# A graph-attention layer and a routed expert layer in one kernel: first loads reordered, the router folded into the projections, the routing steps moved apart

## What is computed

```python
h = (xn @ W).reshape(N, 8, 256)                       # xn = layernorm(x), W 256 x 2048
e = leaky_relu(a_src[src] + a_dst[dst], 0.2)          # a_src, a_dst = h . att, one number per head
alpha = exp(e - max over dst) / sum over dst
x1 = x + segment_sum(h[src] * alpha, dst).mean(heads) + bias
t = layernorm(x1)
probs = softmax(t @ router_w.T)                       # 8 experts, the best two with weights rw
out = x1 + t + sum over the two of rw * (gelu(t @ w1[e] + b1[e]) @ w2[e] + b2[e])
```

## Time and profile before

| What | Value |
|---|---|
| median of 3 runs | 999.45 us |
| lowest and highest | 999.15 and 1000.62 us |
| the profiled execution, its time | 1001.77 us |
| the profiled execution, its span | 1000.0 us |
| busy PE, DVE, POOL, ACT | 680.0, 680.9, 638.1, 355.0 us |
| mean granted clock of PE | 0.806 of full speed |
| bytes moved | 189.66 MB, 190 GB/s |

### The profile page before, as it was taken

How to read it: one execution, slowest core, us unless ns; L and a number is a source line. 1 busy time by engine, 2 the same in 40 slices (tenths; PEclk the granted TensorE clock), 3 DMA queues, 4 the chain that set the end, 5 groups by cost and what they waited for, 6 DMA issues and landing times.

```text
span 1000.0 us, 16168 instructions
## 1 busy us (share of the span) xinstructions
PE 680.0 (68%) x3740; PEld 613.1 (61%) x3741; DVE 680.9 (68%) x1847; ACT 355.0 (35%) x831; POOL 638.1 (64%) x705
## 2 busy tenths in 40 slices
PE   3982011456575454754737876999999998678996
PEld 2981010445475453754627875988888887558995
DVE  6989338657476573865768777557868867765663
ACT  3730012447565344442212210133322322335764
POOL 5777777777777777777777740262245166557776
PEclk9555555669787787876768878999999998789998
DMA  9644064678777676675555572398885761467774
GB/s 347 215 106 112 3 142 111 191 232 298 253 225 243 197 241 212 205 212 162 170 163 154 175 247 95 133 396 305 312 323 211 265 225 58 97 124 109 130 127 59
DMA packets 96988, 189.66 MB, mean 190 GB/s; under 512 B 24743, under 2 KB 54802, under 8 KB 95804
## 3 DMA queue, kind: packets, MB, share of 16 engines
q0 software_dynamic: 31680, 70.52, 29.1%
q1 hardware_dynamic: 50256, 72.93, 21.8%
q10 hardware_dynamic: 14960, 45.16, 11.6%
HBM read 124.74 MB, written 64.74 MB: 189 GB/s over the span
## 4 chain that ended last, share of the span: by engine, by line
PE 37%; POOL 21%; DVE 20%; issue 11%; DMA 6%; DVEq 1%; SPq 1%; POOLq 1%; ACT 1%; ACTq 0%; PEld 0%; PEldq 0%
POOL ring L745 18%; PE banks L1108 16%; PE banks L983 9%; PE banks L1183 3%; PE banks L1167 3%; DMA out<-ring 3%; POOL starts_table L798 2%; PE banks L937 2%; DMA ring<-node_table,idx 2%; DVE banks L1384 1%; PE banks L1128 1%; DVE ring L1406 1%; PE banks L1155 1%; DMA arena<-in_src 1%; PE banks L924 1%
## 5 line engine op out<-in xcount | busy, mean ns | idle before, releaser
L745 POOL DMA_INDIRECT ring<-node_table,idx x392 | 377.3, 963 | 121.5 <-issue 113.9
L983 PE MATMUL banks<-arena,ring 128*128 128x160 f32 x1568 | 263.6, 333 | 37.5 <-ACT banks L1275 20.4
L983 PEld LDWEIGHTS banks<-arena,ring 128*128 128x128 f32 x1568 | 251.8, 217 | 49.5 <-issue 49.2
L1269 ACT COPY arena<-banks 128x400 f32<-128x400 f32 x200 | 88.5, 494 | 304.4 <-PE banks L983 187.5
L1108 PE MATMUL banks<-ring 128*128 128x256 f32 x544 | 122.2, 384 | 0.0
L1108 PEld LDWEIGHTS banks<-ring 128*128 128x128 f32 x544 | 103.6, 192 | 13.9
L859 POOL DMA_INDIRECT out<-ring x56 | 90.0, 1607 | 34.3 <-DMA out<-ring 25.7
L1762 DVE TENSOR_TENSOR arena<-hot,banks 128x640 f32<-128x640 f32 x84 | 64.7, 817 | 36.9 <-PE banks L983 34.6
L1167 PEld LDWEIGHTS banks<-ring 128*128 128x128 f32 x448 | 61.6, 203 | 18.0 <-DVE ring L2030 15.2
L1167 PE MATMUL banks<-ring 128*128 128x128 f32 x448 | 63.7, 289 | 11.7 <-DVE ring L2030 11.7
L990 PE MATMUL banks<-ident,edge_e 128*128 128x128 f32 x25 | 7.1, 413 | 92.4 <-DVEq L1663 92.4
(11 more groups left out here) (414 smaller groups left out, 1146.6 us busy)
## 6 DMA issues: line engine op xcount, KB each, us to landing
agg_table<-arena ACTq DMA_DIRECT2D x100, 400.0 KB
ring<-agg_table SPq DMA_DIRECT2D x25, 1600.0 KB, 8.5
ring<-slot_table SPq DMA_DIRECT2D x56, 130.0 KB, 2.6
ring<-node_table,idx POOLq DMA_INDIRECT x392, 2.8
ring<-in_x SPq DMA_DIRECT2D x8, 640.0 KB, 13.3
arena<-in_L_ffn_w SPq DMA_DIRECT2D x16, 256.0 KB, 8.6
node_table<-ring SPq DMA_DIRECT2D x5, 640.0 KB
ring<-in_L_gnn_W ACTq DMA_DIRECT2D x1, 2048.0 KB, 9.2
```

The lines of the kernel that those rows point to most:

```text
L745: pool.indirect_dma_start(rows[:, slot_of(b), :], None, node_table, bass.IndirectOffsetOnAxis(idx[:, b:b + 1], 0)).then_inc(got[got_of(g)] ...
L983: m = pe.matmul(columns[:, k, bass.ds(at * (UNIT * H), SPREAD * H)], lhs[:, k * P:(k + 1) * P], weights, start=False, stop=True, skip_grou ...
L1269: act.copy(stage[j][:, k * SLOTS * H:(k + 1) * SLOTS * H], views[k]).then_inc(drained, 1)
```

## The change

Four things are changed.

1. **First loads.** W is loaded by SP, in two halves with a semaphore each, after the edges and ahead of x. `att_src` stays on ACT, behind the first DVE memset; `att_dst` goes to SP behind x, and behind it the router's 8 rows. The zeros of `starts_in` are written by ACT (an activation) instead of DVE.
2. **Logits without the normalised tiles.** A router logit is rstd * (x1 . r - mean * sum(r)), and x1 . r is x . r + bias . r + (the tile's sums) . (W r) / 8. So the router's 8 columns stand beside the 8 source columns in `va`, and the first score pass has 16 columns; DVE keeps the last 8 as `x_logits`. W is turned on PE in the opening (32 transposes, copied by ACT), multiplied by the router (32 matmuls of 8 columns), and stands as 8 more columns behind each head's 256 in `W_sb`. `project` has 264 columns, and `add_node` has one more small instruction.
3. **Dropped.** `turn_tn`, `copy_tT`, `router` and the semaphores that order them, in the node stage as well as between the first jobs.
4. **Routing spread out.** `shift_logits` has three instructions more and has its own tile, then the picks at the next, PE's positions after the next again, then `places_in_lists`. Before, shift and picks were one block at a tile and the places came at the next. The sizing of the first jobs goes one tile earlier. For the last five tiles the shift comes before the results of job 0.

The cut diff:

```diff
+            for k in range(2):
+                sp.dma_start(W_in[:, k, :], W[k * P:(k + 1) * P, :]).then_inc(in_W[k], 16)
             sp.wait_ge(x_pad, 1)
...
+            sp.dma_start(att_bc[:, 1, :], att_dst...partition_broadcast(P)).then_inc(in_att[1], 16)
+            sp.dma_start(r_rows, router_w).then_inc(in_router, 16)
             sp.wait_ge(zero_ready, 1)
...
+            sp.dma_start(bias_cols[:, :], gnn_bias.rearrange("(k p) -> p k", p=P), ...).then_inc(in_router, 16)
...
-            sp.dma_start(W_sb[:, :, :], W.rearrange("(k p) n -> p k n", p=P)).then_inc(in_proj_w, 16)
+            for k in range(2):
+                sp.dma_start(W_sb[:, k, :, 0:C], W[k * P:(k + 1) * P, :].rearrange("p (h n) -> p h n", h=H)).then_inc(in_proj_w, 16)
...
+            pool.wait_ge(w_router_done, 1)
             pool.wait_ge(target_scores_stored, 16)
...
             pe.wait_ge(idx_ready, 1)
+            pe.wait_ge(in_router, 16)
+            for k in range(2):
+                pe.transpose(bank[1][:, H + k * NX:H + (k + 1) * NX], r_rows[:, k * P:(k + 1) * P], ident[0:NX, 0:NX])
             mean_va(0)
...
+            pe.wait_ge(blocks_counted, 2 * TILES)
+            pe.wait_ge(x_logits_kept, 1)
+            for i in range(W_PARTS // 4):
+                ...
+                    m = pe.transpose(bank[(0, 2)[i % 2]][:, n * P:(n + 1) * P], W_in[:, k, c * P:(c + 1) * P], ident[:, :])
+            for i in range(W_PARTS // 2):
+                for f in range(2):
+                    pe.matmul(bank[7][:, i * NX:(i + 1) * NX], wT[:, 2 * i + f, :], rT[:, f, :], start=(f == 0), stop=(f == 1))
...
-                        m = pe.matmul(bank[proj_bank(t)][:, 0:D], aggt[...][:, k * H + h, :], W_sb[:, k, h * C:(h + 1) * C],
+                        m = pe.matmul(bank[proj_bank(t)][:, 0:CN], aggt[...][:, k * H + h, :], W_sb[:, k, h, :],
...
                 project(t)
-                for i in turned_after(t):
-                    turn_and_route(i)
...
-            act.dma_start(W_in[:, :, :], W.rearrange("(k p) n -> p k n", p=P)).then_inc(in_W, 16)
-            for a, att in enumerate((att_src, att_dst)):
-                act.dma_start(att_bc[:, a, :], ...).then_inc(in_att[a], 16)
+            act.wait_ge(edges_pad, 1)
+            act.dma_start(att_bc[:, 0, :], att_src...).then_inc(in_att[0], 16)
+            act.wait_ge(zeros_ready, 1)
+            act.activation(starts_in, zeros[0:TURN_ROWS, 0:1].to_broadcast([TURN_ROWS, RUN * H]), ACT.Sign).then_inc(zero_ready, 1)
...
+                link(dve.scalar_tensor_tensor(x_logits[:, rows_of(t), :], bank[proj_bank(t)][:, D:CN], 1.0 / H, x_logits[...], ALU.mult, ALU.add))
...
             def shift_logits(q):
-                dve.wait_ge(logit_done, tiles.stop)
-                scores = bank[6][:, 0:UNROLL * NX].rearrange("p (s e) -> p s e", e=NX)
+                scores = probs[:, :, :]
+                link(dve.tensor_tensor(scores, bc(mean[:, tiles], UNROLL), rT_sum[...], ALU.mult))
+                link(dve.tensor_tensor(scores, x_logits[...], scores, ALU.subtract))
+                link(dve.tensor_tensor(scores, scores, bc(rstd[:, tiles], UNROLL), ALU.mult))
...
+        LAST_Q = TILES // UNROLL - 1
+        SHIFTS = {(q + 1) * UNROLL + (1 if q < LAST_Q - 1 else 0): q for q in range(LAST_Q)}
+        PICKS = {t + 1: q for t, q in SHIFTS.items()}
+        POSITIONS_AFTER = {t + 1: q for t, q in PICKS.items()}
+        PLACES = {t + 1: q for t, q in POSITIONS_AFTER.items()}
```

More of the change, by code:

```diff
@@ L160, in gat_moe_kernel @@
         o += 3 * NB
-        assert o <= RING
+        r_rows = ring[0:NX, o:o + D]
+        o += D
+        assert o <= RING and 2 * H * C <= SLOT0 * ROW
         AGG = 2 * H * P
@@ L409, in gat_moe_kernel @@
         in_x = [sem(f"in_x{i}") for i in range(TILES // UNROLL)]
-        in_edges, in_W, in_small = sem("in_edges"), sem("in_W"), sem("in_small")
+        in_edges, in_small = sem("in_edges"), sem("in_small")
+        in_W = [sem(f"in_W{k}") for k in range(2)]
         in_att = [sem(f"in_att{a}") for a in range(2)]
@@ L478, in y_landed @@
             return 16 * (j // Y_RING + 2)
[L480 to L492, removed]
-                done += n
-            return range(0)
-        POSITIONS_AFTER = {2 * UNROLL - 1: 0, 3 * UNROLL - 1: 1, 4 * UNROLL - 1: 2, 5 * UNROLL - 3: 3}
+        LAST_Q = TILES // UNROLL - 1
[3 more added lines that the diff above has]
+        PLACES = {t + 1: q for t, q in POSITIONS_AFTER.items()}
+        assert max(PLACES) == TILES - 2 and FIRST_TILES + UNROLL not in (*SHIFTS, *PICKS, *PLACES)
         POSITIONS, COUNTS = slice(256, 256 + UNROLL * NX), slice(384, 384 + NX)
@@ L1201, in _ @@
             up(1)
-            for t in range(TILES - UNROLL, TILES - 2):
-                turn_and_route(t)
             turn_xs(2)
             down(0)
-            turn_and_route(TILES - 2)
-            turn_and_route(TILES - 1)
             for j in range(1, JOBS):
@@ L1241, in _ @@
                 count_blocks(n)
+            for i in range(2 * H * C // (4 * P)):
+                act.wait_ge(w_turned, i + 1)
+                act.copy(wT[:, 4 * i:4 * i + 4, :].rearrange("p i n -> p (i n)"), bank[(0, 2)[i % 2]]).then_inc(wT_ready, 1)
             for h in range(H):
@@ L1340, in _ @@
             gelus(0)
-            for t in range(TILES - UNROLL, TILES - 2):
-                copy_tT(t)
             copy_xsT(2)
             gelus(1)
-            copy_tT(TILES - 2)
-            copy_tT(TILES - 1)
             exps(TILES // UNROLL - 1)
@@ L1521, in _ @@
             scale_scores(1)
+            dve.wait_ge(in_router, 16 * 2)
+            for k in range(2):
+                link(dve.tensor_scalar(va[:, k, 0:H], rT[:, k, :], bias_cols[:, k:k + 1], None, ALU.mult))
+            dve.sem_inc(bias_rows_ready, 1)
             link(dve.tensor_copy(extras[:, :], extra_f[:, :]))
```

176 lines of the change are left out of this document (88 added, 88 removed).

## The result

The changed kernel took 995.18 us in the median of 7 runs (994.89 to 997.65), beside 999.39 for the kernel before on the same chip: a ratio of 0.9963 [0.9954, 0.9973], 4.2 us less, where 8.8 had been forecast. On another occasion it was 995.26 (6 runs) against 998.51, 0.9962 [0.9947, 0.9976]. The range held it and the sign was right; the size was a little under half of what was said.

A forecast was written before the change was run, and what follows sets the result against it. PE was taken to bound the node stage, with DVE setting its end after the change. Opening +1.0, node stage -8.5 and turn -1.3 gave -8.8 us from the 999.45 median: 990.6 us, range 981 to 998.

The forecast's parts named there:

- The opening: First loads to first gather: router's rows land at about 24.7 us, gathers begin near 58.4, 1.0 us later.
- the us that was counted for completion: Opening: one us added for completion in the landing time of the router's rows, about 24.7 us.
- The early bound of this term: Opening: if the router's rows are there in time, the gathers start 5 us earlier instead of 1.0 later.
- that rival: Opening: the router's rows come in time, gathers start 5 us earlier, 984.6 us; chance 0.15.
- The node stage: The 25 projections: `add_node(24)` done 190.7 us into the stage instead of 199.2, a gain of 8.5 us.
- DVE as the bound: Node stage from tile 14's `add_node`: DVE needs 76.9 us against PE's 71.3, so DVE sets the end at 185.7.
- an allowance of 5 for waits: Node stage: 5 us, bounds 0 and 11, for late tile loads, expert weights and another slow projection.
- a rule that I set aside: DVE's new shifts, read from SBUF, held up by GpSimd: 15 instructions, up to 0.6 us each, 9 us; counted as none.
- the two long projections: Node stage, PE: slow projections after waits for DVE, about 1.8 us more than neighbours, were to go.
- The rival "slower": Node stage: late tile loads and late DVE steps cost up to 26 us over PE's pace, 1005 us; chance 0.07.
- The turn: Node stage to jobs: DVE's 2.01 us wait goes, three instructions (0.7) come, last places 1.3 us earlier.
- The base: Whole kernel: terms read from an execution of 1001.77 us; the difference taken to the median of 999.45.

The follow-up runs named there:

- rows_first_b: Changed kernel with the router's rows loaded on ACT's queue right behind the first attention vector, second run: 988.16 us, 0.9897 of the kernel before.
- no_adds: Changed kernel without POOL's additions of the normalised rows to x for tiles 10 to 19: 0.9854 of the kernel before, on a longer occasion.
- before_c: The kernel before, unedited, run again for a profile: 999.59 us, ratio 0.9999.
- after_again: The changed kernel, unedited, run again on another occasion: 995.26 us, 0.9962 of the kernel before.
- one_block: Changed kernel with the routing of five tiles put back in one block, router still folded in: 1009.10 us, 1.0102 of the kernel before.
- order_alone_d: The kernel before with only the new order of first loads, router as it was: 995.25 us, 0.9960 of the kernel before.
- before_again: The kernel before, unedited, run again on a longer occasion: ratio 0.9999.

## Why the prediction was right or wrong

**The opening: the step that failed.** It was to cost 1.0 us and cost 4.4. The mechanism was the right one (PE held at mean_va(0) by the rows, the gathers by the scores); its size was off in each link. The rows were to land at 24.7, by 7.8 MB and about 1 us of POOL's transfers at 376 GB/s; they landed at 27.1, when 9.0 MB had moved (359 GB/s over the 25 us from 2 to 27). Of these, 7.8 are the loads ahead of the rows, 0.4 are POOL's, and 0.8 are of what SP issues behind the rows, the table of zeros and the target scan, which move beside them. Those 0.8 MB are 2.2 us at 359 GB/s and the lower rate is 1.0 more; the us that was counted for completion is not seen on top. Together that is the 2.4 us, to rounding. From landing to first product 2.1 were counted and 2.8 passed (0.7), the pass took 27.0 in place of 26.7 (0.3), and store and first gather 0.2 more. The sum, 3.6, carries the forecast from 58.4 to 62.0.

The larger fault is one of reading. With the forecast's 4.9 us from scores to first gather, the scores of the kernel before, ready at 51.10, would have let the gathers begin at 56.0, and they began at 57.44: 1.4 us of slack. The forecast used up all of it for rows 2.4 us late, and so every further us of their landing was a us of the end, while the landing was an estimate with no margin in the sum. The early bound of this term was 5 us earlier, "with the rows there in time", and of that the kernel could have had 3.2 us against the mean of before at the first gather (54.50 by rows_first_b), for one line of code. Moving the rows by one place moved PE's start by what the bytes cost, so order of issue did decide here to within a us. The Trainium skill, "DMA: Bandwidth & Descriptors", section "Queues, rings and completion order", which the prediction put beside that rival, says that completion is not in order of issue for one issuing engine; the runs show nothing of the small load overtaking the large ones on its queue.

**The node stage: right, in part by luck.** 8.5 us were forecast and 8.3 measured; add_node(24) was to end 190.7 us into the stage and ends at 190.3 and 189.6 (its start and 0.9 for it). Its steps: projections of 7.12 us (7.13 forecast), no L1119 and L1128, DVE without a pause of over half a us from tile 14 on but for one of 1.1 at 829, PE waiting ahead of the positions after tile 18, all as written. DVE as the bound is shown by both sides: PE's waits moved brought nothing, DVE's stalls removed brought 6 us and PE's own 180.4. But DVE bounds by these stalls: without them its last `add_node` ends 183.9 us into the stage, and PE doesn't stand.

The 190.7 was made of 108.8 us to the end of `add_node(14)`, 76.9 of work on DVE from there, and an allowance of 5 for waits, of the tiles' loads above all. Measured are 110.8, then 79.4 and 78.8 in the two profiles, and from tile 14 no wait for a load: the allowance was filled by 2.0 us from before tile 14 and by instructions held up by POOL's additions, 6.0 us of them in all. The forecast held about 3.0 us of that kind without knowing it, since the sizing of jobs in the earlier trace rows (7.7 us, where no_adds has 4.8) ran beside additions too, as DVE's timeline of the kernel before shows:

```profile
774.35 0.78 DVE L1959 TENSOR_SCALAR job_rev<-job_tmp 128x11 f32<-128x11 f32 x1
```

Less these, its sum of DVE's own work is 73.9 us, and no_adds measures 73.3. What it left out are the picks, 3.1 us. For them a rule that I set aside was right: the Trainium skill, "SBUF — State Buffer", section "Who interferes with whom", says that a VectorE instruction with two inputs in SBUF waits for a GpSimd instruction that reads SBUF, and that a reduction never does. The trace agrees: 0.54 to 0.77 for TENSOR_TENSOR in the rows above, 0.20 for TENSOR_REDUCE between them, and 0.20 for all in no_adds. I looked only at whether the shifts would meet POOL and not at where the moved picks would; they were moved from 818.7 to 808.5, onto additions (809.10 to 814.26) that in the kernel before had ended at 818.55. And the two long projections that the prediction put down to a wait (1.8 us each) are not tied to one: before_c has the waits and none of them, and the changed kernel has one in each profile, once behind the wait of 3.02 us and once, in after_again, behind that of 1.72 (9.01 us at 783.82). Counting them as dropped was wrong, though the DVE bound made it of no account.

What the forecast never priced by itself is the spreading: 14 us by one_block, perhaps 2.4 of them from its order at tile 22. Folding the router in without it gives 1009, slower than the kernel before. The rival "slower" had this mechanism, one late DVE step and a late load after it, and gave 26 us over PE's pace; it came true in one_block, not in the change.

**The turn: wrong in one term.** 1.3 us were forecast, 2.0 for DVE's wait less 0.7 for three instructions. The wait did go; the three took 1.6 us, again for POOL's additions, which leaves 0.4. The first pair of profiles shows that (19.7 and 19.4 us), the second pair nothing (19.7 and 19.9), so that 0.4 itself is not clear of the difference between profiles.

**The base.** The terms were read from one execution of 1001.77 us, 2.3 above the median. By the ledger the miss adds up as follows: of the 8.8 us, 3.4 went in the opening, 0.2 in the stage and 1.3 in the turn, and 1.8 and 0.3 came that nothing had forecast, which gives the 6.0 between the spans. The profiles differ by 6.0 us where the medians differ by 4.2; both profiles of before (999.9 and 1000.0) sit some 2 us over what their medians leave for a span, those of the changed kernel within half a us. Of the 1.8 us less between first gather and first projection, some may be just that. order_alone_d, which has the new order of loads and not the router's part, has 581.9 and so has it too: it is not the router's. What it is stays open.

## What to carry to other kernels

A small load whose consumer heads a chain without slack belongs ahead of the large ones; here its landing went by the bytes ahead of it, with 0.8 MB of what was issued later on top. Where DVE bounds a stage, see which of its instructions with SBUF inputs run beside POOL's, at the new times after a move and not at the old ones, and whether a row that a price is taken from is held up already; a per-partition scale and bias on an idle ACT can take POOL's place. Split a long routing step before folding work into what feeds it, since a step that outlasts the lead of the loads comes back as a wait for a load.

## What was not expected of the hardware

CAST and TENSOR_SCALAR with a single input in SBUF were held up like the two-input ones, by POOL's additions at 767 to 769 in the changed kernel, where their neighbours took 0.17 (the same section of the Trainium skill, "SBUF — State Buffer", "Who interferes with whom", says that both operations can contend with GpSimd when they run in a mode that takes both ports, if their operands meet its conditions; which mode these ran in no trace shows, and I had taken two inputs for the condition):

```profile
766.18 0.17 DVE L1978 SCALAR_TENSOR_TENSOR job_tmp<-job_tmp 128x11 f32<-128x11 f32 x1
766.38 0.78 DVE L1979 TENSOR_SCALAR job_tmp<-job_tmp 128x11 f32<-128x11 f32 x1
767.20 0.77 DVE L1980 CAST job_row<-job_tmp 1x11 int32<-1x11 f32 x1
```

Without the additions the same two take 0.17 and 0.16 us (no_adds). The first instruction that is held starts up to 0.7 us ahead of the first addition's record, here 766.38 against 767.06; why is not shown.

In two projections of one execution of the kernel before PE's granted clock falls for a while to the 1.2 GHz level (0.54 from 806.19 to 809.60), and in none of another (1.00), behind waits of 0.5 to 1.0 us in both: 197.7 against 195.3 us for the same stage. And on the longer occasions the same program took some 14.5% more, with DVE, ACT and POOL as busy as ever (DVE 680.6 us in before_again against 680.9) and waits of this kind (in all, times, longest) in the view of waits of before_again:

```profile
ACT arena L1269 <- remote: 95.5, 16, 11.2
```
